# Product keys: one head's mask made on GpSimd from ScalarE's copy, four heads turned singly

## The chip, the cores and the metric

The kernel runs on one core of a Trainium2 chip. The metric is the device time of one execution in microseconds. A core has five engines with queues of their own: TensorE (PE; its weight loads are shown as PEld), VectorE (DVE), ScalarE (ACT), GpSimd (POOL) and SyncE (SP). They work in order, each on its own queue, and wait for each other by semaphores. Only TensorE writes the banks of PSUM here, GpSimd can't read them, and VectorE and ScalarE can.

## The reference

Twelve layers act one after the other on x, 2 x 1024 tokens of 128 numbers. The change touches the first and the third, which are the same layer, product keys:

```python
def _L0_ffn_ref(x, norm_w, wq, keys, expert_down, expert_up):   # HEADS 8, K 16, NUM_KEYS 32
    x_norm = x * rsqrt(mean(x * x) + EPS) * norm_w
    q = (x_norm @ wq).reshape(B, T, HEADS, 2, DIM_KEY)
    sim = einsum('bthpd,hkpd->pbthk', q, keys)
    s1, i1 = top_k(sim[0], K)
    s2, i2 = top_k(sim[1], K)
    all_scores = (s1[..., :, None] + s2[..., None, :]).reshape(B, T, HEADS, K * K)
    final_scores, pk = top_k(all_scores, K)
    final_idx = take_along_axis(all_idx, pk)
    hidden = gelu(einsum('btd,bthkd->bthk', x_norm, expert_down[final_idx]))
    hidden = hidden * relu(final_scores)
    return einsum('bthk,bthkd->btd', hidden, expert_up[final_idx])
```

The kernel gathers nothing. For each token and head it forms all 32 x 32 = 1024 sums of two similarities, finds the sixteenth best as a threshold, keeps the sums at or above it (a mask) and adds the eight heads' masked sums. The result, 1024 weights per token, multiplies the gelu of x times all of expert_down, and that goes through expert_up.

## The kernel before

The layer is `product_key_ffn`. It works on 16 tiles (`NT`) of 128 tokens, one after the other, and each engine has a `period(i, ...)` that lists its work for tile i in order, with the work for the tiles ahead and the tile behind in between. All order is written out by hand; loops (`Fori`) run over pairs of tiles, so that every second period of VectorE ends with a jump.

For one head h of tile i:

- TensorE, `sum_halves` (line 506): the 1024 sums, in the PSUM pair of banks h % 2. It waits until the mask of head h - 2 has read the pair.
- ScalarE, `read_sums` (620): copies the sums to `sums_sb`, buffer h % 2 (the trace's pk_sums).
- VectorE, `mask` (722): `chosen[h] = (sums in PSUM >= least2) * sums_sb`, one instruction.
- The heads are then added and turned on TensorE, `combine` (513): eight transposes per call accumulate in two banks. For heads 0 and 1, 2 and 3, 4 and 5, GpSimd adds two heads first, `pair` (425), and the sum is turned once; heads 6 and 7 are turned singly. That makes five calls per tile. ScalarE reads the result out, `read_added` (627), and GpSimd multiplies it by the gelus, `weight` (433).

For the threshold of tile i + 1, during tile i: VectorE finds the best keys of each head (`find_best`, 684, after masks 0 and 1), GpSimd forms the candidates (`add_candidates`, 406 to 419), VectorE finds the top eight (`find_top`, 700, after masks 3 and 4), takes them out (`leave_top_out`, 705, after masks 5 and 6), and after mask 7 `find_rest` finds the next eight (710) and writes the threshold:

```python
nc.vector.tensor_scalar(least2[:, odd, :], top[:, :, PK_TOP - 1], 0.0, PK_UNDER, ALU.max, ALU.mult)   # line 712
nc.vector.drain()
```

GpSimd's order in a period is: candidates of i + 1 (waits for the best keys of all heads), pair 0, weight of i - 1, take of i + 2 (394), pair 1, pair 2, low split of i + 2 (`split_low`, 399, which waits for ScalarE's copy of the similarities and feeds the transposes `turn`, 480, early in the next period).

## Time and profile before

| | us |
|---|---|
| median of 3 runs | 2503.75 (2501.33 to 2503.94) |
| the profiled execution | 2503.85, its span 2502.1 |
| first product-key stage | 48 to 355 |
| second product-key stage | 596 to 907 |
| busy in the whole span: PE, DVE, ACT, POOL | 2042.6, 1768.6, 1272.0, 1177.2 |
| mean granted TensorE clock | 0.912 |

The span is the time from the first to the last instruction. Busy times are of one execution. An instruction's start and duration are given in us from the start of the span; what stands in square brackets behind it is the idle time of the engine before it and what ended it. A granted clock of 1.00 is 2.4 GHz, one of 0.50 is 1.2 GHz.

### The profile page before, as it was taken

What the parts mean: (1) busy time and instruction counts of PE and PEld (TensorE: products, weight loads), DVE (VectorE), ACT (ScalarE), POOL (GpSimd) and SP (SyncE); (2) the same over time, 40 slices, a digit from 0 to 9 for tenths busy, and PEclk for the clock granted to TensorE, in tenths of its full rate; (3) what the DMA queues carried; (4) which work ended last, traced back from release to release, by engine and by line L of the source; (5) the groups of instructions that cost most, each with busy time, mean ns of one, the idle gap of its engine ahead of it and who ended that gap; (6) DMA issues with size and microseconds to landing.
All of it is one profiled execution on the core that took longest, in us unless ns stands there. A gap on an engine that the chain in (4) does not pass through costs nothing. (4 is left out here: it accounts for less than half of the span.)

```text
span 2502.1 us, 39069 instructions
## 1 busy us (share of the span) xinstructions
PE 2042.6 (82%) x11750; PEld 1625.5 (65%) x11775; DVE 1768.6 (71%) x4657; ACT 1272.0 (51%) x2389; POOL 1177.2 (47%) x1051
## 2 busy tenths in 40 slices
PE   4888859994888869976997998988983579999745
PEld 3666656663666658854886885667872468888634
DVE  4999953447999967657766765667667668787575
ACT  3666646653666645543555553335542257776321
POOL 3777751002776746531554653003541388887013
PEclk9999989996999979987997998998996789999978
DMA  3000000000000000001000000000000000000000
GB/s 110 1 0 0 0 15 1 0 0 0 1 0 0 0 1 1 1 5 54 1 1 1 1 1 27 1 6 4 1 1 0 1 10 4 5 6 0 19 0 17
DMA packets 16203, 18.64 MB, mean 7 GB/s; under 512 B 2208, under 2 KB 14048, under 8 KB 16096
## 3 DMA queue, kind: packets, MB, share of 16 engines
q1 hardware_dynamic: 16096, 17.35, 2.3%
q8 instruction: 50, 0.82, 0.1%
q14 instruction: 57, 0.47, 0.1%
HBM read 16.30 MB, written 1.05 MB: 7 GB/s over the span
## 5 line engine op out<-in xcount | busy, mean ns | idle before, releaser
L925 POOL TENSOR_TENSOR unit_hid_low<-unit_hid,unit_hid_high 128x512 fp32r<-128x512 f32 x272 | 351.6, 1293 | 329.9 <-ACT unit_hid_high L1103 329.3
L722 DVE SCALAR_TENSOR_TENSOR pk_chosen<-bank,pk_least,pk_sums 128x1024 f32<-128x1024 f32 x256 | 325.3, 1277 | 43.1 <-ACT pk_sums L620 26.0
L620 ACT COPY pk_sums<-bank 128x1024 f32<-128x1024 f32 x256 | 258.6, 1016 | 179.9 <-PE bank L506 174.8
L506 PE MATMUL bank<-pk_pick,pk_sim_both 128*128 128x512 f32 x512 | 197.3, 469 | 103.7 <-DVE pk_chosen L722 103.0
L425 POOL TENSOR_TENSOR pk_chosen<-pk_chosen 128x1024 f32<-128x1024 f32 x96 | 226.7, 2377 | 7.6 <-DVE pk_chosen L722 7.6
L978 PE MATMUL bank<-unit_x_high,units_high 128*128 128x512 f32 x544 | 219.2, 403 | 0.0
L979 PE MATMUL bank<-unit_x_low,units_high 128*128 128x512 f32 x544 | 218.5, 402 | 0.0
L980 PE MATMUL bank<-unit_x_high,units_low 128*128 128x512 f32 x544 | 217.8, 400 | 0.0
L1103 ACT CAST unit_hid_high<-unit_hid 128x512 fp32r<-128x512 f32 x272 | 167.2, 615 | 43.9 <-DVE unit_hid L1230 24.3
L506 PEld LDWEIGHTS bank<-pk_pick,pk_sim_both 128*128 128x128 f32 x512 | 82.5, 201 | 157.4 <-DVE pk_chosen L722 147.4
L513 PE MATMUL bank<-ident,pk_chosen 128*128 128x128 f32 x1280 | 175.0, 283 | 1.3 <-DVE pk_chosen L722 1.3
L513 PEld LDWEIGHTS bank<-ident,pk_chosen 128*128 128x128 f32 x1280 | 157.9, 146 | 23.9 <-issue 2.2
L1096 ACT ACTIVATE unit_gact<-bank,units_small 128x512 f32<-128x512 f32 x136 | 93.5, 689 | 124.3 <-PE bank L980 123.3
L1096 ACT ACTIVATE unit_gact<-bank 128x512 f32<-128x512 f32 x136 | 81.2, 599 | 128.4 <-PE bank L980 128.3
L1217 DVE SCALAR_TENSOR_TENSOR unit_prod<-bank,units_small,unit_gact 128x512 f32<-128x512 f32 x136 | 102.0, 750 | 62.4 <-ACT unit_gact L1096 60.2
L1220 DVE TENSOR_TENSOR unit_prod<-bank,unit_gact 128x512 f32<-128x512 f32 x136 | 93.9, 690 | 65.0 <-PE bank L980 62.1
L2670 POOL TENSOR_TENSOR dh_la<-dh_la_tok,causal 128x1024 fp32r<-128x1024 f32 x64 | 120.1, 1897 | 4.6
L1230 DVE SCALAR_TENSOR_TENSOR unit_hid<-unit_prod,units_small,bank 128x512 f32<-128x512 f32 x136 | 101.8, 748 | 29.0 <-PE bank L1013 24.3
L980 PEld LDWEIGHTS bank<-unit_x_high,units_low 128*128 128x128 f32 x544 | 105.3, 194 | 24.2
L979 PEld LDWEIGHTS bank<-unit_x_low,units_high 128*128 128x128 f32 x544 | 105.3, 194 | 24.0
L978 PEld LDWEIGHTS bank<-unit_x_high,units_high 128*128 128x128 f32 x544 | 105.6, 194 | 23.5
L1013 PE MATMUL bank<-unit_comb,units_pick 128*128 128x512 f32 x272 | 109.5, 405 | 7.1 <-DVE unit_comb L1203 7.1
(387 smaller groups left out, 5158.9 us busy)
## 6 DMA issues: line engine op xcount, KB each, us to landing
raw<-in_geglu_units SPq DMA_DIRECT2D x3, 774.0 KB, 7.5
raw<-in_swiglu_units SPq DMA_DIRECT2D x3, 768.0 KB, 7.6
dh_w_next<-in_de_w SPq DMA_DIRECT2D x8, 192.0 KB, 2.3
out_x<-x_res SPq DMA_DIRECT2D x1, 1024.0 KB, 5.1
raw<-in_geglu_units SPq DMA_DIRECT2D x1, 967.5 KB, 11.1
raw<-in_swiglu_units SPq DMA_DIRECT2D x1, 960.0 KB, 11.2
pk_down<-in_pk_downT SPq DMA_DIRECT2D x1, 512.0 KB, 5.2
pk_up<-in_pk_up SPq DMA_DIRECT2D x1, 512.0 KB, 6.5
```

The source lines that it names most:

```text
L425: nc.gpsimd.tensor_tensor(chosen[:, 2 * c, :], chosen[:, 2 * c, :], chosen[:, 2 * c + 1, :], ALU.add).then_inc(paired.sem, 1)
L506: ins = nc.tensor.matmul(sums_ps[:, 2 * b + e, :], both[:, odd, h, :], pk.pick[:, e * PK_K // 2:(e + 1) * PK_K // 2, :].rearrange("p i j - ...
L513: ins = nc.tensor.matmul(comb_ps[j // 4][:, (j % 4) * P:(j % 4 + 1) * P], chosen[:, h, j * P:(j + 1) * P], k.ident[:], start=(first and j ...
L620: nc.scalar.copy(sums_sb[:, b, :].rearrange("p (e n) -> p e n", e=2), sums_ps[:, 2 * b:2 * b + 2, :]).then_inc(sums_out.sem, 1)
L722: nc.vector.scalar_tensor_tensor(chosen[:, h, :].rearrange("p (e n) -> p e n", e=2), sums_ps[:, 2 * b:2 * b + 2, :], least2[:, odd, h:h + ...
L925: nc.gpsimd.tensor_tensor(hid_low[:, i % HB, :], hid[:, i % HB, :], hid_high[:, i % HB, :].bitcast(FP32), ALU.subtract).then_inc(hidden.se ...
L978: nc.tensor.matmul(to, w_hi, x_high[:, tokens], start=True, stop=False)
L979: nc.tensor.matmul(to, w_hi, x_low[:, tokens], start=False, stop=False)
L980: return nc.tensor.matmul(to, w_lo, x_high[:, tokens], start=False, stop=True)
L1096: nc.scalar.activation(gact[:, i % 2, :], gate_ps[i % 2], m.func, bias=b).then_inc(gated.sem, 1)
L1103: nc.scalar.copy(hid_high[:, i % HB, :], hid[:, i % HB, :]).then_inc(rounded.sem, 1)
L2670: ins = nc.gpsimd.tensor_tensor(la[:, q % 2, i, :, :, :].rearrange("p t h n -> p (t h) n"), la_tok[:, i, :, :].rearrange("p t h -> p (t h) ...
```

## The change

Head 4's mask leaves VectorE. ScalarE copies head 4's sums to a third buffer of `sums_sb`, and GpSimd makes the mask from that copy alone, in two instructions with a drain between (`mask_head`), behind a dummy addition of two elements and in the place of pair 2. Heads 4 and 5, which were added and turned once, are turned singly, which makes six `combine` calls per tile: heads 6 and 4 of the tile behind at head 0, head 7 at head 1, pair 0 at head 4, head 5 at head 6, pair 1 at head 7. The sums of head 6 now wait for ScalarE's copy of head 4 in place of a mask. The clearing of `least2` becomes a clearing of eight numbers of `top`. The waits count accordingly.

```diff
-PK_PAIRS = PK_H // 2
+PK_PAIRS = 2
+PK_POOL_HEAD = 4
+PK_MASKED = PK_H - 1
+PK_COMBINED = PK_H - PK_PAIRS
...
-        sums_sb = k.scratch(ctx, "pk_sums", [P, 2, PK_E])
+        sums_sb, unused = k.scratch(ctx, "pk_sums", [P, 3, PK_E]), k.scratch(ctx, "pk_unused", [P, 2])
...
+        buffer_of = lambda h: 2 if h == PK_POOL_HEAD else h % 2
+        masked_to = lambda i, h: PK_MASKED * i + (h + 1 if h < PK_POOL_HEAD else h)
...
+            def mask_head(i, odd):
+
+                if since(i, 1):
+                    pool.wait_ge(combined.sem, combined.at(PK_COMBINED * (i - 1) + 5))
+                pool.wait_ge(least_ready.sem, least_ready.at(i + 1))
+                pool.wait_ge(sums_out.sem, sums_out.at(PK_H * i + PK_POOL_HEAD + 1))
+                nc.gpsimd.tensor_tensor(unused[:], k.ones[:, 0:2], k.ones[:, 0:2], ALU.add)
+                nc.gpsimd.tensor_scalar(chosen[:, PK_POOL_HEAD, :], sums_sb[:, 2, :],
+                                        least2[:, odd, PK_POOL_HEAD:PK_POOL_HEAD + 1], None, ALU.is_ge)
+                nc.gpsimd.drain()
+                nc.gpsimd.tensor_tensor(chosen[:, PK_POOL_HEAD, :], chosen[:, PK_POOL_HEAD, :], sums_sb[:, 2, :],
+                                        ALU.mult).then_inc(masked_pool.sem, 1)
...
                 pair(i, 1)
-                pair(i, 2)
+                mask_head(i, odd)
...
-                if since(i, 1) or h >= 2:
-                    pe.wait_ge(masked.sem, masked.at(n - 1))
+                if h == PK_POOL_HEAD + 2:
+                    pe.wait_ge(sums_out.sem, sums_out.at(n - 1))
+                elif h >= 2:
+                    pe.wait_ge(masked.sem, masked.at(masked_to(i, h - 2)))
+                elif since(i, 1):
+                    pe.wait_ge(masked.sem, masked.at(masked_to(i - 1, PK_H + h - 2)))
...
                         if not first:
-                            combine_pair(i - 1, 2)
+                            combine_head(i - 1, PK_H - 2)
+                            combine_head(i - 1, PK_POOL_HEAD)
...
                     if h == 6:
-                        combine_head(i, PK_H - 2)
+                        combine_head(i, PK_POOL_HEAD + 1)
...
                 act.wait_ge(sums.sem, sums.at(PK_H * i + h + 1))
+                if h == PK_POOL_HEAD and since(i, 1):
+                    act.wait_ge(masked_pool.sem, masked_pool.at(i))
-                nc.scalar.copy(sums_sb[:, b, :].rearrange("p (e n) -> p e n", e=2),
+                nc.scalar.copy(sums_sb[:, buffer_of(h), :].rearrange("p (e n) -> p e n", e=2),
...
-                    nc.vector.memset(least2[:, odd, :], 0.0)
+                    nc.vector.memset(top[:, 0, 0:8], 0.0)
...
-                nc.vector.tensor_scalar(least2[:, odd, :], top[:, :, PK_TOP - 1], 0.0, PK_UNDER, ALU.max, ALU.mult)
+                nc.vector.tensor_scalar(least2[:, odd, :], top[:, :, PK_TOP - 1], 0.0, PK_UNDER, ALU.max,
+                                        ALU.mult).then_inc(least_ready.sem, 1)
...
                 for h in range(PK_H):
-                    mask(i, odd, h)
+                    if h != PK_POOL_HEAD:
+                        mask(i, odd, h)
```

## Rows read from the trace of the kernel before

**Rows 1.** Busy time by stage: window, length, each engine's busy us (instructions), clock, DMA

```profile
48.00:355.00 307.00, 249.26 (x1552) 205.24 (x1552) 270.10 (x909) 192.32 (x249) 213.18 (x182) 0.94 0.00 0
596.00:907.00 311.00, 249.97 (x1558) 204.76 (x1556) 274.94 (x943) 195.37 (x253) 214.49 (x184) 0.94 0.00 0
```

**Rows 2.** The page's costliest groups: count, busy us, mean ns, idle before

```profile
L722 DVE SCALAR_TENSOR_TENSOR pk_chosen<-bank,pk_least,pk_sums 128x1024 f32<-128x1024 f32 x256 | 325.3, 1277 | 43.1 <-ACT pk_sums L620 26.0
...
L425 POOL TENSOR_TENSOR pk_chosen<-pk_chosen 128x1024 f32<-128x1024 f32 x96 | 226.7, 2377 | 7.6 <-DVE pk_chosen L722 7.6
```

**Rows 3.** The timeline of VectorE, one period: start us, us, instruction, idle before

```profile
199.19 1.28 DVE L722 SCALAR_TENSOR_TENSOR pk_chosen<-bank,pk_least,pk_sums 128x1024 f32<-128x1024 f32 x1 [0.27 <-issue]
...
204.09 2.46 DVE L722 SCALAR_TENSOR_TENSOR pk_chosen<-bank,pk_least,pk_sums 128x1024 f32<-128x1024 f32 x2
...
209.45 1.28 DVE L722 SCALAR_TENSOR_TENSOR pk_chosen<-bank,pk_least,pk_sums 128x1024 f32<-128x1024 f32 x1
...
214.95 1.30 DVE L710 MAX8 pk_top<-pk_cand_rest 128x8 f32<-128x87 f32 x8
216.33 0.74 DVE L712 TENSOR_SCALAR pk_least<-pk_top 128x8 f32<-128x8 f32 x1
217.77 1.28 DVE L722 SCALAR_TENSOR_TENSOR pk_chosen<-bank,pk_least,pk_sums 128x1024 f32<-128x1024 f32 x1 [0.69 <-issue]
```

**Rows 4.** The timeline of GpSimd in the same period

```profile
203.25 0.63 POOL L406 TENSOR_TENSOR pk_cand<-pk_sims,pk_best 128x256 f32<-128x256 f32 x1 [4.36 <-DVE pk_best L684]
...
206.21 2.37 POOL L425 TENSOR_TENSOR pk_chosen<-pk_chosen 128x1024 f32<-128x1024 f32 x1
...
211.12 4.70 POOL L425 TENSOR_TENSOR pk_chosen<-pk_chosen 128x1024 f32<-128x1024 f32 x2
215.78 1.27 POOL L399 TENSOR_TENSOR pk_sim_parts<-pk_sims,pk_sim_parts 128x512 fp32r<-128x512 f32 x1
```

**Rows 5.** VectorE's groups up to 906 us, line 712

```profile
L712 DVE TENSOR_SCALAR pk_least<-pk_top 128x8 f32<-128x8 f32 x32 | 20.6, 643 | 2.5
```

**Rows 6.** The timeline at the end of the following period, all engines

```profile
235.32 1.28 POOL L399 TENSOR_TENSOR pk_sim_parts<-pk_sims,pk_sim_parts 128x512 fp32r<-128x512 f32 x1 [0.92 <-ACT pk_sim_parts L603]
...
235.97 0.66 DVE L712 TENSOR_SCALAR pk_least<-pk_top 128x8 f32<-128x8 f32 x1
...
236.90 1.28 DVE L722 SCALAR_TENSOR_TENSOR pk_chosen<-bank,pk_least,pk_sums 128x1024 f32<-128x1024 f32 x1 [0.27 <-issue]
```

**Rows 7.** The timelines of GpSimd and VectorE at the last threshold

```profile
324.10 4.72 POOL L425 TENSOR_TENSOR pk_chosen<-pk_chosen 128x1024 f32<-128x1024 f32 x2
...
329.57 0.17 DVE L712 TENSOR_SCALAR pk_least<-pk_top 128x8 f32<-128x8 f32 x1
330.05 1.28 DVE L722 SCALAR_TENSOR_TENSOR pk_chosen<-bank,pk_least,pk_sums 128x1024 f32<-128x1024 f32 x1 [0.30 <-ACT pk_sums L620]
```

**Rows 8.** The timeline of all engines, TensorE's and ScalarE's instructions

```profile
201.10 1.04 PE L513 MATMUL bank<-ident,pk_chosen 128*128 128x128 f32 x8
...
207.53 1.01 ACT L620 COPY pk_sums<-bank 128x1024 f32<-128x1024 f32 x1 [0.34 <-PE bank L506]
...
219.10 0.87 PE L506 MATMUL bank<-pk_pick,pk_sim_both 128*128 128x512 f32 x2 [1.92 <-DVE pk_chosen L722]
...
219.78 1.91 PE L513 MATMUL bank<-ident,pk_chosen 128*128 128x128 f32 x8
```

**Rows 9.** TensorE's granted clock by windows of 19 us (the second view: PE alone)

```profile
198.00:217.00 19.00, 15.88 (x109) 13.10 (x106) 18.01 (x63) 12.99 (x17) 14.49 (x13) 1.00 0.00 0
217.00:236.00 19.00, 15.78 (x95) 12.90 (x94) 16.70 (x61) 11.83 (x16) 13.15 (x13) 0.91 0.00 0
...
690.00:709.00 19.00, 15.77 (x97) 0.91 0.00 0
```

**Rows 10.** GpSimd's groups by shape: nearest prices

```profile
L412 POOL TENSOR_TENSOR pk_cand<-pk_best 128x64 f32<-128x64 f32 x64 | 18.0, 299 | 0.0
...
L1950 POOL COPY ro_xb<-x_norm_t 128x1024 f32 x2 | 2.1, 1038 | 13.7 <-PE bank L1974 13.7
...
L2542 POOL TENSOR_SCALAR_AFFINE_SELECT de_mask<-dg_zeros 128x512 bf16<-128x512 f32 x1 | 0.6, 634 | 0.2 <-issue 0.2
```

More of the change, by code:

```diff
@@ L39 @@
     pk_sums pk_sums_out pk_masked pk_paired pk_combined pk_added_out pk_hidden pk_gelu pk_weighted
-    pk_product pk_product_out pk_folded pk_scaled
+    pk_product pk_product_out pk_folded pk_scaled pk_masked_pool pk_least
 """, """
@@ L359, in product_key_ffn @@
              "pk_second", "pk_cand", "pk_sums", "pk_sums_out", "pk_masked", "pk_paired", "pk_combined", "pk_added_out",
-             "pk_hidden", "pk_gelu", "pk_weighted", "pk_product", "pk_product_out")
+             "pk_hidden", "pk_gelu", "pk_weighted", "pk_product", "pk_product_out", "pk_masked_pool", "pk_least")
     (tile_in, sim, sim_out, sim_high, sim_low, sim_t, sim_t_out, best_ready, second, cand_ready, sums, sums_out, masked,
-     paired, combined, added_out, hidden, gelu, weighted, product, product_out) = [k.counter(n) for n in names]
+     paired, combined, added_out, hidden, gelu, weighted, product, product_out, masked_pool, least_ready) = [k.counter(n) for n in names]
     NCH = PK_E // P
@@ L422, in pair @@
             def pair(i, c):
-                pool.wait_ge(masked.sem, masked.at(PK_H * i + 2 * c + 2))
+                pool.wait_ge(masked.sem, masked.at(masked_to(i, 2 * c + 1)))
                 nc.gpsimd.tensor_tensor(chosen[:, 2 * c, :], chosen[:, 2 * c, :], chosen[:, 2 * c + 1, :],
                                         ALU.add).then_inc(paired.sem, 1)
+            def mask_head(i, odd):
[9 more added lines that the diff above has]
+                                        ALU.mult).then_inc(masked_pool.sem, 1)
             def weight(i, odd):
@@ L519, in combine_pair @@
             def combine_pair(i, c):
-                pe.wait_ge(paired.sem, paired.at((PK_PAIRS - 1) * i + c + 1))
+                pe.wait_ge(paired.sem, paired.at(PK_PAIRS * i + c + 1))
                 if c == 0:
@@ L526, in combine_head @@
             def combine_head(i, h):
-                pe.wait_ge(masked.sem, masked.at(PK_H * i + h + 1))
+                if h == PK_POOL_HEAD:
+                    pe.wait_ge(masked_pool.sem, masked_pool.at(i + 1))
+                else:
+                    pe.wait_ge(masked.sem, masked.at(masked_to(i, h)))
                 combine(h, last=(h == PK_H - 1))
@@ L592, in _ @@
             period(NT - 1, 1, last=True, ahead=False)
-            combine_pair(NT - 1, 2)
+            combine_head(NT - 1, PK_H - 2)
+            combine_head(NT - 1, PK_POOL_HEAD)
             combine_head(NT - 1, PK_H - 1)
@@ L717, in mask @@
                 b = h % 2
-                if since(i, 1) and h in (0, 2, 4, 7):
-                    dve.wait_ge(combined.sem, combined.at((PK_PAIRS + 1) * (i - 1) + {0: 1, 2: 3, 4: 4, 7: 5}[h]))
+                if since(i, 1) and h in (0, 2, 6, 7):
+                    dve.wait_ge(combined.sem, combined.at(PK_COMBINED * (i - 1) + {0: 1, 2: 3, 6: 4, 7: 6}[h]))
                 dve.wait_ge(sums_out.sem, sums_out.at(n + 1))
@@ L765, in product_key_ffn @@
         s.passed(NT)
-    for s in (sums, sums_out, masked):
+    for s in (sums, sums_out):
         s.passed(NT * PK_H)
-    paired.passed(NT * (PK_PAIRS - 1))
-    combined.passed(NT * (PK_PAIRS + 1))
+    masked.passed(NT * PK_MASKED)
+    for s in (masked_pool, least_ready):
+        s.passed(NT)
+    paired.passed(NT * PK_PAIRS)
+    combined.passed(NT * PK_COMBINED)
     for s in (sim_t, sim_t_out, hidden, gelu):
```

2 lines of the change are left out of this document (1 added, 1 removed).

## The prediction

> **What bounds the kernel now.** I read the stages first. The change touches only the two product-key stages, and together they take 618 of the 2502 us of span [rows 1]. In both VectorE is the busiest engine (270 of 307 us, 275 of 311 us), so the page invites the sentence "VectorE sets the pace". The groups of the page give the prices: one head mask on VectorE 1277 ns, one pair sum on GpSimd 2377 ns [rows 2]. A tile has eight masks and three pair sums.
>
> Next the timeline of one tile in the steady part, engine by engine. I count from the start of the tile's mask 0, at 199.19; all times written +x are us after it. The next tile's mask 0 starts at 217.77, so this period is 18.58 us [rows 3]. VectorE has little idle time in it; 0.69 us of it lie before the next mask 0. GpSimd starts the candidates at +4.06, as soon as the eighth head's best keys are there, then runs without a pause through pair 0, weight, take, pair 1, pair 2 and the low split, which it starts at +16.59 and ends at 217.05, +17.86 [rows 4].
>
> The reader is to look at what stands at that time on VectorE: the small operation on line 712, the threshold of the next tile, starts at 216.33 and ends at 217.07, with the end of GpSimd's split. It handles 128x8 elements. Of its 32 instances the mean is 643 ns [rows 5]. In the following period it ends at 236.63 and the split ends at 236.60 [rows 6]. Near the end of the stage there is no split, GpSimd has been idle since 328.82, and line 712 takes 0.17 us [rows 7]. So it holds off until GpSimd's running instruction is over, and this costs some 0.57 us here, beyond its own work. The masks (one input in PSUM) last 1.27 to 1.28 us beside a busy or an idle GpSimd [rows 2 to 4]: they don't wait in this way. The Trainium skill, "SBUF — State Buffer", section "Who interferes with whom", has this as an exclusive lock of a shared port pair, taken for a whole instruction by a VectorE tensor_scalar in a two-port mode or by a GpSimd instruction, whichever was first; the 0.17 against 0.74 us agree.
>
> The period is thus closed by a loop over two engines: mask 0, best keys, GpSimd's whole queue, line 712, mask 0. VectorE without that hold would be done with line 712 at +17.31 (starts at +17.14, lasts 0.17), GpSimd lets it go at +17.88.
>
> A third thing is TensorE's clock. It idles 1.92 us before the first sums of the next tile at 219.10, so since 217.18, and then runs at its low level (1.2 GHz): eight turns take 1.91 us, 1.04 at the high one (2.4 GHz) [rows 8]. A stretch of this kind shows as 0.91 in a window of 19 us, and one without it as 1.00; six tiles of the first stage have one and five of the second [rows 9]. A period with such a stretch is 19.13 us (217.77 to 236.90): line 712 starts at +18.20 in it instead of +17.14 [rows 6].
>
> **VectorE's part of the change.** Mask 4 goes: -1.28 us per tile, 32 tiles, 41 us, were VectorE alone the bound. It isn't all to be had even there. Mask 5 needs ScalarE's copy of head 5, which ran at 207.53 to 208.54 [rows 8], and in front of that copy the work of the extra turn (below) moves ScalarE's queue some 0.3 us later. So mask 5 can start at about +9.65 in place of +10.26 [rows 3], the rest follows at its old spacing, and line 712 is ready to start at about +16.55 (+17.14 less 0.6). The fill of the top tile's first eight numbers in place of the threshold's is the same small memset: nothing.
>
> **GpSimd's part.** One pair sum goes (2.38 us). In come a dummy addition of 2 elements, the compare, a drain and a multiplication. The multiplication has the pair sum's shape and inputs: 2.37. The dummy: 64 elements take 0.30 us [rows 10], back to back less; 0.2. The drain: 0.15, my estimate from steps between GpSimd's small instructions; both may be off by 0.1 together. The compare has one tensor input, and no row shows a tensor_scalar on GpSimd. Lower bound: the copy of 128x1024, 1.04 us; upper: the two-input rate, 2.38 [rows 2, 10]. The one other compare, the affine select of 128x512, takes 0.63 us, about 1.1 for twice the elements, so I take 1.05 for start to start. New is then 3.77 for 2.38, the queue grows by 1.4 us per tile. GpSimd is idle for 4.36 us before the candidates [rows 4], so by load alone this is free.
>
> By place it isn't. Pair 1 ends, and the dummy starts, at +14.28 (211.12 + 2.35). Dummy to +14.48, compare to +15.53, drain to +15.68, multiplication to +18.05. Line 712 becomes ready at +16.55, in the middle of the multiplication, and must stand until +18.05. Before, it was let go at +17.88. The mask taken off VectorE gives nothing: its 0.6 us turn into more waiting on the same loop, and the loop is 0.17 us longer. In sentences of their own: the same page's rule, that the second to come waits for the whole instruction, and the skill's warning in "Perfetto Trace Analysis", section "Optimizing Scalar/DVE Operations", that moving work between these two engines might not help because they share a port, both speak against this change. By load without the rule the stages would lose some 1.2 us per period.
>
> **TensorE's part.** Six groups of eight turns per tile for five: +0.87 us of issue. The two turned singly at head 0 come before the turns of the similarities and before the sums of head 3, so these are 0.87 us later. At the high clock this is covered: the sums of head 3 end at about +4.9, ScalarE's copy about +6.0, and mask 3 starts at +6.1 anyway, back to back behind mask 2 at 204.09, +4.90 [rows 3]. At the low clock it isn't. The chain from the first sums to the sums of head 4 is 0.87 us longer and its 0.1 us of slack is left in place of 1; the 1.7 us that a low stretch costs TensorE come through whole, where before 1.06 did (18.20 less 17.14): mask 5 is as late as before, and line 712 gets ready at about +18.17, no earlier than today's +18.20. By then the multiplication is over (+18.05) and the low split has begun: it holds line 712 until about +19.3. Before: +18.86. So a period with a low stretch is 0.4 us longer. The gap in which TensorE idles grows too (last multiplications over at +17.4, next sums at +19.7 to +20.1: 2.3 to 2.7 us for about 1.4, without a low stretch after it, and 1.9, with one), which speaks for at least as many low stretches. The head 6 sums wait for ScalarE's copy and not for a mask: earlier, covered. ScalarE's copy of head 4 waits for the last tile's multiplication, done by +0.1 of its period: nothing. No DMA is moved.
>
> **The sum.** Between line 712's end and mask 0 lie 0.69 us at a loop's end, else 0.27 [rows 3, 6]. Thirteen periods per stage are in the steady part, six with the loop's end. Before, in the first stage: 7 x 18.17 (17.88 + 0.02 + 0.27) + 6 x 18.58 + 6 x 0.96 for low stretches (19.13 less 18.17) = 244.4; in the second, with five, 243.5. After: 7 x 18.34 + 6 x 18.76 = 240.9, and low stretches that come out at 19.55 or 19.97, +1.21 each; I take five to six of them, +6.5: 247.4, so +3.0 and +3.9 us. The next to last tile has no split, and line 712 lasted 0.17 us there [rows 7]; now it waits for the multiplication to +18.05: +0.7 each. The last tile: its final turns wait for GpSimd's last product, about where the last pair sum ended: 0 to 0.3. Sum: 3.0 + 3.9 + 1.4 + 0.3, about +8.6 us. Against the profiled execution: span 2502.1, time 2503.85 (1.75 around it), the median 2503.75. Forecast 2512.
>
> **The rivals.**
> *The compare is slow enough to let line 712 through (faster).* If it takes 1.95 us or more, the multiplication hasn't begun when line 712 is ready; line 712 goes between them, at about +16.87 with a compare of 2.37, and mask 0 follows at +17.14 or +17.56. TensorE's gap falls to 1.1 to 1.5 us, so no low stretches. 7 x 17.14 + 6 x 17.56 = 225.3, 19 us less per stage: 2465. It decides at +16.55. For: the two-input rate of all the neighbours. Against: copy and select at about 1 ns per element.
> *The product doesn't hold line 712 (faster).* The same gain, about 2464. Against it: in 28 of the 32 instances line 712 ended with GpSimd's instruction, and in the other four GpSimd was idle [rows 3 to 7].
> *A compare of 1.3 to 1.9 us (slower).* Every 0.1 us moves the multiplication's end, and the loop, by 0.1 us. At 1.85 the loop is at +18.85, 0.95 us over before, and low stretches hide in it: 13 x 19.3 = 251, +7 per stage, +1.6 each for the next to last tile: 2521. The Trainium skill, "GPSIMD Engine Reference", section "Performance pitfalls for Q7 kernels", has compare bodies at 2.03 cycles per element unless unrolled, 1.03 if so; by its figures an estimate of the compare would be 1.8 or 0.95 us.
> *Nothing to be measured.* Line 712 in low stretches gets ready by +18.0 instead of +18.17 and slips in ahead of the split. Then these cost nothing, 2 x (241 + 0.7) against 488: about 2500 to 2505.
>
> **How the numbers follow.** The forecast's case 0.36, the slower compare 0.17, nothing to be measured 0.22, the two faster ones 0.25 (0.20 and 0.05). About 0.2% (5 us) is what a measurement of this kernel tells from no change. The likeliest case has 2505 to 2518 as its range. Both signs hold much of the chance, so the range goes from the fast compare to the slow one: 2463 to 2526. Slower 0.53, same 0.22, faster 0.25.
>
> **What the profile will show.** Right: line 712 ends with the end of GpSimd's multiplication, with a mean duration near 1.5 us and not 0.64; mask 5 starts about 0.6 us earlier in the tile, mask 0 no earlier; VectorE's busy time apart from line 712 falls by 41 us and the span does not. The compare is between 1.0 and 1.15 us. Low stretches at half of the tiles or more, with line 712 ending with the low split. Wrong: if line 712 ends ahead of the multiplication, I have mis-sized the compare or VectorE's chain; if it ends inside it, the hold is not what I take it for; if TensorE idles at the turn of head 4 at the tile's start, waiting for GpSimd's product, the wait is on another engine than I say.

## The result and the profile after

The changed kernel takes 2527.53 us (median of 5 runs, 2517.78 to 2531.99), the one before 2502.9 (5 runs, 2495.05 to 2503.94): ratio 1.0103, 95% interval 1.0075 to 1.0131. It is slower by 1.0%, 24.6 us by these medians, where 2512 was forecast, and just above the range forecast (2463 to 2526). The profiled execution has a span of 2525.8 us.

The page's costliest groups and its total of busy time (engine, busy us, share, instructions):

```profile
PE 2072.3 (82%) x12006; PEld 1663.4 (66%) x12031; DVE 1757.3 (70%) x4625; ACT 1263.8 (50%) x2389; POOL 1275.7 (51%) x1115
...
L752 DVE SCALAR_TENSOR_TENSOR pk_chosen<-bank,pk_least,pk_sums 128x1024 f32<-128x1024 f32 x224 | 285.0, 1276 | 78.7 <-ACT pk_sums L649 64.5
```

GpSimd's groups up to 935 us, by shape:

```profile
L440 POOL TENSOR_SCALAR pk_chosen<-pk_sums,pk_least 128x1024 f32<-128x1024 f32 x32 | 91.2, 2851 | 0.0
...
L443 POOL TENSOR_TENSOR pk_chosen<-pk_chosen,pk_sums 128x1024 f32<-128x1024 f32 x32 | 75.3, 2354 | 4.7
```

VectorE's groups up to 935 us, the threshold (line 712 before, 741 now):

```profile
L741 DVE TENSOR_SCALAR pk_least<-pk_top 128x8 f32<-128x8 f32 x32 | 47.6, 1486 | 2.5
```

Against [rows 2, 5]: 32 masks are gone from VectorE, 325.3 to 285.0 us, as the change says, and the idle time ahead of the masks rose from 43.1 to 78.7. The threshold rose from 643 to 1486 ns, 27 us in all, for 128x8 elements each time. And the compare, line 440, takes 2851 ns, not the 1.05 us that I took, and longer than either of my bounds. The product (2354 ns) is as forecast.

The timeline of the changed kernel, one period of the first stage from mask 0 at 209.72 to mask 0 at 230.33, 20.61 us, for [rows 3, 4, 8] (start us, us, instruction, idle before it):

```profile
209.72 1.28 DVE L752 SCALAR_TENSOR_TENSOR pk_chosen<-bank,pk_least,pk_sums 128x1024 f32<-128x1024 f32 x1 [0.29 <-issue]
...
211.05 0.73 PE L528 MATMUL bank<-pk_pick,pk_sim_both 128*128 128x512 f32 x2 [2.69 <-DVE pk_chosen L752]
...
211.62 3.45 PE L535 MATMUL bank<-ident,pk_chosen 128*128 128x128 f32 x16
...
220.81 1.28 DVE L752 SCALAR_TENSOR_TENSOR pk_chosen<-bank,pk_least,pk_sums 128x1024 f32<-128x1024 f32 x1 [0.92 <-ACT pk_sums L649]
...
224.08 0.20 POOL L439 TENSOR_TENSOR pk_unused<-ones 128x2 f32<-128x2 f32 x1
...
224.25 2.85 POOL L440 TENSOR_SCALAR pk_chosen<-pk_sums,pk_least 128x1024 f32<-128x1024 f32 x1
...
227.25 2.35 POOL L443 TENSOR_TENSOR pk_chosen<-pk_chosen,pk_sums 128x1024 f32<-128x1024 f32 x1
...
227.70 1.92 DVE L741 TENSOR_SCALAR pk_least<-pk_top 128x8 f32<-128x8 f32 x1
229.55 1.27 POOL L404 TENSOR_TENSOR pk_sim_parts<-pk_sims,pk_sim_parts 128x512 fp32r<-128x512 f32 x1
230.33 1.28 DVE L752 SCALAR_TENSOR_TENSOR pk_chosen<-bank,pk_least,pk_sums 128x1024 f32<-128x1024 f32 x1 [0.71 <-issue]
```

The product begins at 227.25, the threshold becomes ready at 227.70, 0.45 us too late, and ends with the product (229.60 and 229.62). Sixteen turns take 3.45 us, against 1.91 in the period below, so TensorE began this tile at its low level (1.2 GHz). I call that a low start; a high start is one at 2.4 GHz.

The same kernel in the second stage, from mask 5 to the end of one period, and the mask 0 that follows, with TensorE's rows behind it:

```profile
671.39 1.28 DVE L752 SCALAR_TENSOR_TENSOR pk_chosen<-bank,pk_least,pk_sums 128x1024 f32<-128x1024 f32 x1 [0.67 <-ACT pk_sums L649]
...
676.39 2.85 POOL L440 TENSOR_SCALAR pk_chosen<-pk_sums,pk_least 128x1024 f32<-128x1024 f32 x1
...
678.27 0.99 DVE L741 TENSOR_SCALAR pk_least<-pk_top 128x8 f32<-128x8 f32 x1
679.38 2.35 POOL L443 TENSOR_TENSOR pk_chosen<-pk_chosen,pk_sums 128x1024 f32<-128x1024 f32 x1
679.98 1.28 DVE L752 SCALAR_TENSOR_TENSOR pk_chosen<-bank,pk_least,pk_sums 128x1024 f32<-128x1024 f32 x1 [0.72 <-issue]
...
681.32 0.73 PE L528 MATMUL bank<-pk_pick,pk_sim_both 128*128 128x512 f32 x2 [1.90 <-DVE pk_chosen L752]
681.88 1.91 PE L535 MATMUL bank<-ident,pk_chosen 128*128 128x128 f32 x16
```

Mask 0 before that is at 661.95, so the period is 18.03 us. The threshold is ready 16.32 us into it, while the compare still runs. It is held for 0.99 us, but it gets in at the compare's end (679.24), ahead of the product. Mask 5 starts 9.44 us into this period (10.26 before) and 11.09 into the one above. The kernel thus has two modes, and TensorE's granted clock tells them apart. In the first mode every tile has a low start and the product holds the threshold, in the second every tile has a high start and only the compare does. The first two windows below lie in the first mode (0.91), the last two in the second (1.00); columns are length, TensorE's busy us with instructions, clock, DMA:

```profile
120.00:140.00 20.00, 16.86 (x107) 0.91 0.00 0
200.00:220.00 20.00, 16.85 (x107) 0.91 0.00 0
...
660.00:680.00 20.00, 17.22 (x122) 1.00 0.00 1
700.00:720.00 20.00, 17.40 (x125) 1.00 0.00 0
```

| | before | after, second mode | after, first mode |
|---|---|---|---|
| period, us (alternating) | 18.17 / 18.58; 19.13 with a low start | 17.61 / 18.02 | 20.2 / 20.6 |
| threshold ready, us into it | 17.15; 18.21 low | 16.32 | 17.98 |
| threshold done | 17.89; 18.87 low | 17.32 | 19.90 |

All of the first stage's steady part is in the first mode: thirteen periods, from mask 0 at 67.16 to mask 0 at 332.05, in 264.9 us, where the kernel before took 244.6. The second stage has eight periods in the second mode (644.34 to 786.86, 17.8 on average) and then changes over for good: its thirteen take 244.3 us, before 243.4. The threshold of the next to last tile, which before lasted 0.17 us [rows 7], is held for 1.57 by the product in both stages, and that period is 2.3 us longer. The last tile is 1.1 us longer in the first stage and 1.9 in the second: its final turns wait 1.56 and 1.57 us for GpSimd's product of head 4 (until 368.50 and 925.08). The stages, from the first mask 0 to the addition behind the last tile, are 329.3 and 308.9 us long where they were 305.5 and 303.9: +23.8 and +5.0. The rest of the kernel is 5 us shorter in this execution, which makes the +23.7 of the spans. That the same kernel ran between 2517.8 and 2532.0 us fits a changeover that comes earlier or later from run to run; only one of those runs has a profile, so this is argued and not shown.

### The profile page after: what moved, and what is told of

Its sections match the earlier page's. It is cut to its first block and busy times, and to the rows that moved or that the text cites. A ratio compares the mean times of both kernels' runs of the same rounds, so it can differ in the third digit from the quotient of the medians.

```text
span 2525.8 us, 39661 instructions
## 1 busy us (share of the span) xinstructions
PE 2072.3 (82%) x12006; PEld 1663.4 (66%) x12031; DVE 1757.3 (70%) x4625; ACT 1263.8 (50%) x2389; POOL 1275.7 (51%) x1115
## 3 DMA queue, kind: packets, MB, share of 16 engines
HBM read 16.30 MB, written 1.05 MB: 7 GB/s over the span
## 5 line engine op out<-in xcount | busy, mean ns | idle before, releaser
L752 DVE SCALAR_TENSOR_TENSOR pk_chosen<-bank,pk_least,pk_sums 128x1024 f32<-128x1024 f32 x224 | 285.0, 1276 | 78.7 <-ACT pk_sums L649 64.5
L535 PE MATMUL bank<-ident,pk_chosen 128*128 128x128 f32 x1536 | 222.8, 299 | 3.1 <-POOL pk_chosen L443 3.1
L535 PEld LDWEIGHTS bank<-ident,pk_chosen 128*128 128x128 f32 x1536 | 203.2, 156 | 26.5 <-issue 3.7
L430 POOL TENSOR_TENSOR pk_chosen<-pk_chosen 128x1024 f32<-128x1024 f32 x64 | 152.1, 2376 | 5.8 <-DVE pk_chosen L752 5.8
L1013 PEld LDWEIGHTS bank<-unit_x_low,units_high 128*128 128x128 f32 x544 | 105.2, 193 | 23.8
```

The costliest lines, as they stand in the source:

```text
L430: nc.gpsimd.tensor_tensor(chosen[:, 2 * c, :], chosen[:, 2 * c, :], chosen[:, 2 * c + 1, :], ALU.add).then_inc(paired.sem, 1)
L535: ins = nc.tensor.matmul(comb_ps[j // 4][:, (j % 4) * P:(j % 4 + 1) * P], chosen[:, h, j * P:(j + 1) * P], k.ident[:], start=(first and j ...
L752: nc.vector.scalar_tensor_tensor(chosen[:, h, :].rearrange("p (e n) -> p e n", e=2), sums_ps[:, 2 * b:2 * b + 2, :], least2[:, odd, h:h + ...
L1013: nc.tensor.matmul(to, w_hi, x_low[:, tokens], start=False, stop=False)
```

## The experiments

Each edit is against the changed kernel unless it says that it is against the one before. Ratios, with 95% intervals, are to the kernel before as it was timed anew beside each group of runs. It took 2500.45 us beside the threshold on ScalarE, the product in four pieces, the twelve multiplications and the turns alone; 2504.29 beside the same threshold in the kernel before, the prices, the compare left out and the eight multiplications; and 2500.29 beside the rest.

### Is it the hold? The threshold on ScalarE

```diff
-                nc.vector.tensor_scalar(least2[:, odd, :], top[:, :, PK_TOP - 1], 0.0, PK_UNDER, ALU.max,
-                                        ALU.mult).then_inc(least_ready.sem, 1)
...
+            def threshold(i, odd):
+
+                act.wait_ge(rest_ready.sem, rest_ready.at(i + 1))
+                nc.scalar.activation(least2[:, odd, :], top[:, :, PK_TOP - 1], ACT.Relu,
+                                     scale=PK_UNDER).then_inc(least_ready.sem, 1)
...
+                    if h == 7 and not last:
+                        threshold(i + 1, 1 - odd)
...
+                if h == 0:
+                    dve.wait_ge(least_ready.sem, least_ready.at(i + 1))
```

The threshold becomes the last instruction of a tile on ScalarE's queue, behind the copy of head 7, and VectorE's mask 0 waits for it.

> The changed kernel, with the threshold (max with 0, times a constant) computed by ScalarE from VectorE's top sixteen, so that no VectorE instruction at this place can be held by GpSimd; compare and product stay as long as they are. Theory A (the hold is what turns GpSimd's queue into time): in low stretches mask 0 follows at about +18.6 or +19.0 in place of +20.2 or +20.6, at the high clock at about +17.0 or +17.4; time 2480 to 2500. Rival B (it is the length of GpSimd's queue, through TensorE waiting for head 4's product or the low split): at least 2515, with TensorE idle in front of head 4's turns.

Measured: 2459.98 us, ratio 0.9840 (0.9820 to 0.9860), better than expected. The timeline of this kernel at the end of a period and the start of the next:

```profile
218.20 2.87 POOL L440 TENSOR_SCALAR pk_chosen<-pk_sums,pk_least 128x1024 f32<-128x1024 f32 x1
...
220.64 0.22 ACT L655 ACTIVATE pk_least<-pk_top 128x8 f32<-128x8 f32 x1
221.07 1.29 DVE L760 SCALAR_TENSOR_TENSOR pk_chosen<-bank,pk_least,pk_sums 128x1024 f32<-128x1024 f32 x1 [0.78 <-ACT pk_least L655]
221.22 2.37 POOL L443 TENSOR_TENSOR pk_chosen<-pk_chosen,pk_sums 128x1024 f32<-128x1024 f32 x1
```

The threshold takes 0.22 us in the middle of GpSimd's compare, and mask 0 starts while GpSimd still has the product to do. Every period of the steady parts is 17.2 to 17.3 us, and no low start is left in them. TensorE never waits for head 4's product there; it does so for 1.55 us in the last tile of each stage. The same edit on the kernel before:

> The kernel before with the one edit of act_after: the threshold is computed by ScalarE. Theory A (GpSimd's low split holds line 712 in the kernel before too, and the changed kernel only lengthens that hold): mask 0 comes at about +17.6 in place of +18.17 and +18.58, TensorE's gap is down to about 1.0 us, so no low stretches; time 2470 to 2480. With it, the worth of the changed kernel's edit free of the hold can be read: act_after's periods were 17.24 us. Rival B (the hold is a cost of the changed kernel alone): 2495 to 2502.

Measured: 2474.32 us, ratio 0.9878 (0.9850 to 0.9905); periods 17.77 and 17.83. So the kernel before, too, had some 30 us to gain. They aren't all the hold. The steady parts of the two stages are 25.4 us shorter (231.5 and 231.1 for 244.6 and 243.4). Eleven low starts that are gone make 10.5 of it; some 5 are the jump at the end of VectorE's loop, which made every second period 0.41 us longer and doesn't show now that mask 0 waits for ScalarE; some 10, about 0.4 us a period, are the hold, net of ScalarE's 0.26 us until it starts the threshold. The edit also takes two drains off VectorE, which no run tests by themselves.

With the threshold on ScalarE in both, the change is to the good, by some 10 us. The medians differ by 14 us (2474 and 2460) but were timed beside different runs of the kernel before; the ratios (0.9878 and 0.9840) give 9.5 us, and their intervals just overlap. In the profiles the steady parts are 14.0 us shorter together, and the last tiles 3.2 longer.

### What holds it? The product in four pieces, and the threshold in eight

```diff
-                nc.gpsimd.tensor_tensor(chosen[:, PK_POOL_HEAD, :], chosen[:, PK_POOL_HEAD, :], sums_sb[:, 2, :],
-                                        ALU.mult).then_inc(masked_pool.sem, 1)
+                for part in range(4):
+                    at = slice(part * PK_E // 4, (part + 1) * PK_E // 4)
+                    ins = nc.gpsimd.tensor_tensor(chosen[:, PK_POOL_HEAD, at], chosen[:, PK_POOL_HEAD, at],
+                                                  sums_sb[:, 2, at], ALU.mult)
+                ins.then_inc(masked_pool.sem, 1)
```

> The changed kernel, with the product on GpSimd in four pieces of 256 columns (about 0.65 us each, 0.2 to 0.3 us more in sum). Theory A (whole instructions hold, VectorE comes in at the end of one): the threshold ends with the piece in which it became ready, at most 0.7 us after +17.98, so low periods of about 18.9 and 19.3, time about 2500 or less. Rival B (GpSimd's queue has to end before the threshold gets in): as the changed kernel or 0.3 us per period over it, 2527 to 2535.

Measured: 2492.29 us, ratio 0.9967 (0.9952 to 0.9982). The timeline where the threshold is late:

```profile
225.92 2.78 POOL L445 TENSOR_TENSOR pk_chosen<-pk_chosen,pk_sums 128x256 f32<-128x256 f32 x4
226.38 0.30 DVE L744 TENSOR_SCALAR pk_least<-pk_top 128x8 f32<-128x8 f32 x1
226.97 1.28 DVE L755 SCALAR_TENSOR_TENSOR pk_chosen<-bank,pk_least,pk_sums 128x1024 f32<-128x1024 f32 x1 [0.29 <-ACT pk_sums L652]
```

The four products together take longer (2.78 for 2.35 us), yet the threshold, 0.46 us behind their start as before, lasts 0.30 us for 1.92: it waits for one piece and not for the product. A period with a low start is 18.56 us in place of 20.2. TensorE's gap behind such a period is only about 1.07 us, and the next tile starts high: seven of the 26 steady periods have a low start, and never two in a row. So with the hold cut short the first mode doesn't lock. One steady period (18.94 us, behind one of 16.79) has TensorE waiting 0.86 us for head 4's product at the tile's start, the wait that the prediction named as its third sign of being wrong; it is the only one in the steady parts of these runs. The other side of the same question: eight thresholds of one column each.

```diff
-                nc.vector.tensor_scalar(least2[:, odd, :], top[:, :, PK_TOP - 1], 0.0, PK_UNDER, ALU.max,
-                                        ALU.mult).then_inc(least_ready.sem, 1)
+                for h in range(PK_H):
+                    ins = nc.vector.tensor_scalar(least2[:, odd, h:h + 1], top[:, h, PK_TOP - 1:PK_TOP], 0.0, PK_UNDER,
+                                                  ALU.max, ALU.mult)
+                ins.then_inc(least_ready.sem, 1)
```

> The changed kernel with the threshold computed on VectorE as before, but in eight instructions of one column each in place of one of eight columns. Theory A (the hold comes with the form that streams one operand through both of VectorE's ports, and one element has no second half): none of the eight is held, each takes 0.07 us or so, the threshold is done by +16.9 at the high clock, periods 17.2 to 17.7, time 2462 to 2480. Rival B (any tensor_scalar from SBUF to SBUF is held, or each of the eight anew between GpSimd's instructions): durations of over 1 us among them, time as the changed kernel or more, 2515 or over.

Measured: 2480.22 us, ratio 0.9912 (0.9886 to 0.9937), at the upper edge of what I expected of theory A (2462 to 2480). The timeline, first a tile with a low start, where the product runs from 85.56 to 87.91, then one with the compare running from 224.67 to 227.52:

```profile
85.56 2.35 POOL L443 TENSOR_TENSOR pk_chosen<-pk_chosen,pk_sums 128x1024 f32<-128x1024 f32 x1
...
86.03 0.58 DVE L742 TENSOR_SCALAR pk_least<-pk_top 128x1 f32<-128x1 f32 x8
...
224.67 2.85 POOL L440 TENSOR_SCALAR pk_chosen<-pk_sums,pk_least 128x1024 f32<-128x1024 f32 x1
...
226.56 0.58 DVE L742 TENSOR_SCALAR pk_least<-pk_top 128x1 f32<-128x1 f32 x8
227.52 1.28 DVE L754 SCALAR_TENSOR_TENSOR pk_chosen<-bank,pk_least,pk_sums 128x1024 f32<-128x1024 f32 x1 [0.38 <-ACT pk_sums L649]
```

Eight instructions on the same engine do the same work in 0.58 us, 0.47 us behind the product's start, where one instruction, 0.45 us behind it, takes 1.92 in the changed kernel. Two low starts are left, in the first steady tile of each stage, and they don't lock. The threshold on VectorE is not held as such: it is this instruction of eight columns that is. The Trainium skill, "SBUF — State Buffer", section "Who interferes with whom", has a VectorE tensor_scalar contend for the port pair shared with GpSimd when it runs in a two-port mode. That a one-column instruction stays out of that mode would fit the page, but no row shows the mode.

### The price of the compare

The kernel before with seven GpSimd instructions added at its end, each three times, in sequence and with no other engine at work:

> The kernel before with a stage added at its end, in which GpSimd alone runs seven operations three times each, on 128x1024 but for one: a copy, is_ge with a constant, is_ge with a per-token threshold, the same on 128x512, a multiplication by a per-token number, is_ge and mult with constants in one instruction, and a subtraction of two tensors. Theory A (the price is that of the compare): the two is_ge forms about 2.85 us, the multiplication about 1.04 us like the copy. Rival B (the price is that of reading the scalar from memory): is_ge with a constant about 1.04, the multiplication about 2.85. Rival C (the price is that of tensor_scalar on GpSimd): all four near 2.85. 512 columns: 1.4 us if it goes by columns.

The timeline of GpSimd in that part:

```profile
2493.86 1.04 POOL L3174 COPY pr_copy<-pr_src 128x1024 f32<-128x1024 f32 x1
2494.87 2.78 POOL L3175 TENSOR_SCALAR pr_imm<-pr_src 128x1024 f32<-128x1024 f32 x1
2497.64 2.84 POOL L3176 TENSOR_SCALAR pr_ptr<-pr_src,pr_lim 128x1024 f32<-128x1024 f32 x1
2500.46 1.56 POOL L3177 TENSOR_SCALAR pr_half<-pr_src,pr_lim 128x512 f32<-128x512 f32 x1
2502.00 2.85 POOL L3178 TENSOR_SCALAR pr_mul<-pr_src,pr_lim 128x1024 f32<-128x1024 f32 x1
2504.82 3.64 POOL L3179 TENSOR_SCALAR pr_two<-pr_src 128x1024 f32<-128x1024 f32 x1
2508.43 1.89 POOL L3180 TENSOR_TENSOR pr_sub<-pr_src 128x1024 f32<-128x1024 f32 x1
```

A compare costs what a multiplication with a per-token value costs (2.84, 2.85), and a constant in place of the value saves 0.06. So neither the compare nor the read of the threshold is what makes it dear, and the other engines don't either: on GpSimd, this tensor_scalar costs 2.7 times the copy, and 1.2 times a product of two tensors. Half the columns take 1.56 us and not 1.42, so by these two rows about 0.3 us of it doesn't go by columns (my estimate). Then the compare left out, with head 4's product kept (this kernel leaves the mask of head 4 out, so it is for timing alone):

```diff
-                nc.gpsimd.tensor_scalar(chosen[:, PK_POOL_HEAD, :], sums_sb[:, 2, :],
-                                        least2[:, odd, PK_POOL_HEAD:PK_POOL_HEAD + 1], None, ALU.is_ge)
-                nc.gpsimd.drain()
-                nc.gpsimd.tensor_tensor(chosen[:, PK_POOL_HEAD, :], chosen[:, PK_POOL_HEAD, :], sums_sb[:, 2, :],
+                nc.gpsimd.tensor_tensor(chosen[:, PK_POOL_HEAD, :], sums_sb[:, 2, :], sums_sb[:, 2, :],
```

> The changed kernel without the compare and its drain: GpSimd multiplies head 4's sums with themselves, so head 4's mask is left out. The hold, the extra turn and the third buffer stay. Theory A (it is the size of the compare, 2.85 us, that puts the product where it holds a late threshold): the product runs from about +14.5 to +16.85, periods about 17.1 and 17.6 us at the high clock, low ones at most 19.1; time 2460 to 2480. Rival B (the extra turn and the low clock make the loss): 2510 or more.

Measured: 2490.6 us, ratio 0.9945 (0.9932 to 0.9959), less gain than expected. The timeline shows why:

```profile
138.35 1.90 POOL L440 TENSOR_TENSOR pk_chosen<-pk_sums 128x1024 f32<-128x1024 f32 x1
...
140.21 1.28 POOL L404 TENSOR_TENSOR pk_sim_parts<-pk_sims,pk_sim_parts 128x512 fp32r<-128x512 f32 x1
140.25 1.27 DVE L738 TENSOR_SCALAR pk_least<-pk_top 128x8 f32<-128x8 f32 x1
```

The queue is shorter by more than the compare, since the product with both inputs the same takes 1.90 us and not 2.35. The product is over at +16.32, just as the threshold gets ready, and the next instruction, the low split, starts 0.04 us ahead of the threshold and holds it for 1.27 in the product's place. In the nine steady periods with a low start (18.9 us) the split holds it too, 0.66 us. Taking work off GpSimd does not remove the hold: what counts is which instruction happens to start just ahead of the threshold.

### TensorE's clock

Zero multiplications into a PSUM bank whose values they don't alter, in TensorE's gap ahead of the next tile's first sums: twelve and then five of them in the changed kernel, eight in the one before. In a trace each shows as two passes.

```diff
+            def fill():
+                for _ in range(12):
+                    nc.tensor.matmul(low_ps[:, 0:P], nothing[:], k.ident[:], start=False, stop=False)
...
-                            multiply(i - 1, (5, 6, 7))
+                            multiply(i - 1, (5, 6))
+                            fill()
+                            multiply(i - 1, (7,))
```

> The changed kernel, with twelve multiplications of a zero tile added on TensorE in the stretch in which it waits for the next tile's threshold (they add zero to a sum that is open anyway). Theory A (the threshold on VectorE is held by GpSimd's product only because the low TensorE clock has made it late: ready at +17.98, the product begins at +17.53; without the low clock it is ready at +16.32 and passes at the compare's end, +17.32): no low stretches in the steady part, every period 17.6 or 18.0 us as in the first eight periods of the second stage, steady part of the first stage from 265 to about 231 us, of the second from 244 to 231; time about 2480, some 1% under the kernel before. Rival B (GpSimd's queue, longer by 3 us, sets the period whatever the clock): periods stay at 20.2 and 20.6, time 2520 to 2530.

Measured: 2503.0 us, ratio 1.0011 (1.0001 to 1.0022). The clock is 1.00 throughout the steady part, and the locked 20.2 us periods are gone, but not the 2480 that I expected. The timeline:

```profile
212.05 2.35 POOL L444 TENSOR_TENSOR pk_chosen<-pk_chosen,pk_sums 128x1024 f32<-128x1024 f32 x1
...
212.39 2.04 DVE L750 TENSOR_SCALAR pk_least<-pk_top 128x8 f32<-128x8 f32 x1
...
212.86 2.84 PE L572 MATMUL bank<-ident,pk_nothing 128*128 128x128 f32 x24
```

The fill lasts 2.8 us, longer than the gap, so that the sums come later with each period: the threshold is ready at 16.32, 17.25, 17.36, 17.80 us in turn. The fourth one falls behind the product's start at the high clock and is held 2.04 us; near the end of the first stage one starts 0.02 us behind the product and takes 2.37, the longest in these runs. It isn't the clock that holds, but lateness; the low clock is one way to be late. With five:

> As awake_after with five multiplications of the zero tile in place of twelve, because each of them takes two passes and twelve took 2.8 us, longer than TensorE's gap at the high clock (1.5 us) and so late themselves; five take about 1.2 us. Theory A (a threshold that is ready before the compare is over passes; the low clock is what makes it late in the changed kernel): no low stretches but perhaps in the first tile, the threshold ready at +16.3, every period 17.6 or 18.0, time 2475 to 2485. Rival B (GpSimd's backlog, 1.2 us over per fast period, comes back by way of the low split and makes a threshold late every few tiles, as in awake_after, without any low clock): some periods of 20.5 remain, time 2495 to 2505.

Measured: 2481.75 us, ratio 0.9919 (0.9897 to 0.9942), as expected. All steady periods of both stages are 17.6 or 18.0 us; the timeline has the threshold end with the compare each time:

```profile
223.09 2.86 POOL L441 TENSOR_SCALAR pk_chosen<-pk_sums,pk_least 128x1024 f32<-128x1024 f32 x1
...
224.99 0.98 DVE L750 TENSOR_SCALAR pk_least<-pk_top 128x8 f32<-128x8 f32 x1
...
225.74 1.28 PE L572 MATMUL bank<-ident,pk_nothing 128*128 128x128 f32 x10
226.09 2.37 POOL L444 TENSOR_TENSOR pk_chosen<-pk_chosen,pk_sums 128x1024 f32<-128x1024 f32 x1
```

So 1.3 us of work without use turns the change from 1.0% slower to 0.8% faster. On the kernel before:

> The kernel before with eight multiplications of a zero tile (about 1.0 us) in TensorE's gap. Theory A (its low stretches cost 0.96 us each, eleven in the two stages): every period 18.17 or 18.58, time 2490. Rival B (the added work delays TensorE's next sums as in awake_after, where the threshold was ready at +17.25 in place of +16.32): 2500 or more, with the threshold ready later than +17.15.

Measured: 2502.78 us, ratio 0.9999 (0.9984 to 1.0014). The low starts are gone there too, and the steady parts of the two stages are shorter by 10 us together (238.8 and 238.7 for 244.6 and 243.4), but the median doesn't follow. In the profiled execution the part of the kernel behind the second stage is 5.5 us longer (1602.6 for 1597.1). That part is the same code in all of these kernels but the one with the prices, and its length goes from 1592.4 us (the changed kernel) to that 1602.6, with 1601.9 in a run without any added multiplication (the turns alone), so the 5.5 us need not come of the added work. Why the medians of ten and seventeen runs lie 1.5 us apart and not 10, these runs don't settle.

### The turns alone, and GpSimd's queue

Against the kernel before, pair 2 goes and heads 4 and 5 are turned singly, with all eight masks on VectorE:

```diff
-                pair(i, 2)
...
-                            combine_pair(i - 1, 2)
+                            combine_head(i - 1, 6)
+                            combine_head(i - 1, 4)
...
-                        combine_head(i, PK_H - 2)
+                        combine_head(i, 5)
```

> One part of the change alone, on the kernel before: heads 4 and 5 are turned singly and pair 2 is gone, but all eight masks stay on VectorE. Theory A (the extra turn in front of the similarities' turns costs time only in low stretches): at the high clock the period is 18.0 or 18.4 us (the low split now ends at about +17.75), with a low stretch 19.7 to 20.2 where it was 19.13, because the threshold gets ready some 0.8 us later and the split has moved with ScalarE's copy; time 2497 to 2512. Rival B (the extra turn is covered everywhere): 19.13 stays 19.13 or less, time 2495 to 2502. Rival C (the extra turn makes the changed kernel's loss by itself): about 2525.

Measured: 2503.72 us, ratio 1.0014 (1.0000 to 1.0028), no change to speak of, and within theory A's range. The threshold is ready at +17.45 where it was at +17.15, and the split starts later too; periods are 18.37 and 18.79 (+0.2), against which only one low start is left in each stage's steady part (20.04 us, 0.9 over the 19.13 of before: the extra turn whole). The timeline there:

```profile
233.43 1.28 POOL L400 TENSOR_TENSOR pk_sim_parts<-pk_sims,pk_sim_parts 128x512 fp32r<-128x512 f32 x1 [4.07 <-ACT pk_sim_parts L605]
234.09 0.66 DVE L714 TENSOR_SCALAR pk_least<-pk_top 128x8 f32<-128x8 f32 x1
```

GpSimd had 4.07 us to spare and still held the threshold. Last, the version with the threshold on ScalarE and the copy of the tile (0.3 us) moved from GpSimd to ScalarE as well:

```diff
-                if ahead:
-                    take(i + 2, odd)
...
+                        if ahead:
+                            nc.scalar.copy(xt[:, odd, :], k.xnT[:, bass.ts(i + 2, P)]).then_inc(tile_in.sem, 1)
```

> act_after with one more edit: the copy of the next tile's tokens (0.29 us, 0.25 start to start) goes from GpSimd to ScalarE. Theory A (with the hold gone, GpSimd's queue of some 17.0 us is what sets act_after's 17.24 us): periods about 17.0 us, 7 us less in all, time about 2453. Rival B (VectorE's own chain or TensorE's sums set it): 17.24 stays, time 2460, or more by ScalarE's added 0.25 us in front of a sums copy.

Measured: 2464.21 us, ratio 0.9851 (0.9829 to 0.9873); not the 2453 of theory A. The periods stay at 17.2 to 17.3, but for one low start at the beginning (18.67), though the compare now ends at +17.05 in place of +17.30. Once the threshold is not held, GpSimd's queue doesn't set the period. This version and the one without the copy moved are the fastest, 1.5 and 1.6% under the kernel before, and their intervals overlap. Against the changed kernel the 2459.98 us are 2.7% less (from 2527.53, timed at another time).

## Why the prediction was wrong, step by step

**The steps that failed** are two, and the loss needs both. The first is the compare's price: "The compare has one tensor input [...] Lower bound: the copy of 128x1024, 1.04 us; upper: the two-input rate, 2.38". It measured 2.85 us, and 2.78 to 2.85 with no other engine at work. I took two rows of other operations for bounds, and they weren't bounds: the operation with one tensor input costs more than the one with two. Had I left the upper end open, I should have asked what 3 us would do. In a sentence by itself: the estimate of 0.95 or 1.8 us from the figures of the Trainium skill, "GPSIMD Engine Reference", section "Performance pitfalls for Q7 kernels" (its 1.03 or 2.03 cycles per element at that page's clock of 1.2 GHz come to 0.88 or 1.73), is as far off, and the measurement decides.

The price alone doesn't give the loss. With 2.85 us in my own sum the threshold passes at the compare's end, +17.33, and thirteen periods of 17.60 and 18.02 without low starts make 231.3 us a stage, about 2479 in all, faster than before; the run with five zero multiplications, which is just that case, took 2481.75. The second step that failed is what the rival of the slow compare goes on with: "TensorE's gap falls to 1.1 to 1.5 us, so no low stretches". The gap was 1.48 and 1.90 us in turn in the second mode, and one of 1.89 was followed by a low start. For a compare as long as this I priced neither that gap nor a hold by the product behind a low start.

**What the price did.** The product started at +17.5 and not at +15.68. I had worked out that a compare of 1.95 us or more lets the threshold through, and put that on the faster side, 2465. At the high clock this is what happened: ready at +16.32 (I had +16.55), done at the compare's end, +17.32, periods of 17.61 and 18.02. In a low period the threshold is ready at +17.98 (I had +18.17), 0.45 us behind the product's start, and is held to +19.90. A period is 20.2 or 20.6, where I had 19.55 or 19.97 for a hold by the split.

**The number of low starts.** I took five to six in thirteen periods. It was thirteen in the first stage and five in the second, and the first mode keeps itself going: the hold makes mask 0 late, TensorE idles 2.69 and then 3.12 us ahead of the sums (1.92 before, [rows 8]), starts low, so the next threshold is late and is held again. The run with the product in four pieces bears this out: held for one piece, a low period is never followed by another. I had 247.4 us for the steady part of either stage; it was 264.9 in the first, and 244.3 in the second, where eight short periods pay for five long ones. For the next to last tile I had +0.7 and it was +2.3, for the last 0 to 0.3 and it was 1.1 and 1.9. What I named as speaking "for at least as many low stretches" was the gap of 2.3 to 2.7 us; what it would do to the next tile I didn't price.

**Right.** That the threshold is held for the length of GpSimd's running instruction and sets the period: with it on ScalarE, both kernels gain, and with the product in pieces or the threshold in eight, the changed one does. That VectorE's 41 us aren't to be had: its masks fell by 40.3 us while the threshold rose by 27 and the idle time ahead of the masks by 35.6. That the 0.87 us of turns come through whole after a low start: ready is 1.66 us later there (17.98 less 16.32), where before it was 1.06, and I had 1.7. The small costs (0.20 us for the dummy instruction, some 0.15 for the drain, 2.35 for the product). The turns are not quite covered at the high clock, as the run with them alone shows: +0.3 us on the threshold, about what I had given to ScalarE's copy.

**Right by luck.** The side, slower: the case that I put there (a compare of 1.05 us, the product holding at every clock, +0.17 us a period) didn't occur, and the compare that did occur I had on the faster side. And the sign "a mean duration near 1.5 us" for the threshold: it was 1.49, but as a mixture of about 1.0 and 1.92, with none near 1.5 but the 1.57 of the next to last tiles. The sign of being wrong that came true is the first that I named, line 712 ending ahead of the multiplication, in the eight periods of the second mode.

**Of the rivals,** the slow compare that lets the threshold through came true in the second mode, and the first mode has the forecast's hold by the product, though only behind a low start, and for longer. The time is a mixture: in this execution 18 steady periods in the first mode and 8 in the second.

**Open.** What decides when the second mode changes over. The period from 768.84 to 786.86 looks like the seven before it, and TensorE's gap behind it, below, like the one at 681.32 (1.90 us, and sixteen turns in 1.91).

```profile
788.19 0.86 PE L528 MATMUL bank<-pk_pick,pk_sim_both 128*128 128x512 f32 x2 [1.89 <-DVE pk_chosen L752]
788.86 3.47 PE L535 MATMUL bank<-ident,pk_chosen 128*128 128x128 f32 x16
```

No run shows why one started low and the other didn't. The kernel before has the same: 1.98 us at 106.91 and a high start, 1.92 at 219.10 and a low one. In the profiles of this document but that of the prices, the first and last tile of each stage left out, the low starts stand behind gaps of 1.82 to 3.14 us, and the high ones behind gaps of up to 2.30.

## What to carry to other kernels

Before moving work between VectorE and GpSimd, look for a small VectorE instruction whose duration varies and whose end falls on the end of a GpSimd instruction; if it is on the loop that sets the period, give it to ScalarE or to a form that isn't held first, and only then count what the move saves. A price that no row shows has no upper bound from other operations: measure it alone, or carry the case above your bound through the loop. And when a wait makes TensorE's gap longer and a low start makes the wait, price the two as a loop that keeps itself going, and not the single stretch.

## What the runs showed of the hardware

GpSimd's tensor_scalar on 128x1024 float32 takes 2.8 us with one operation and 3.64 with two, against 1.04 for a copy, 1.89 for a difference of a tensor with itself and 2.35 for a product of two tensors. VectorE's threshold of 128x8 takes 0.17 us free and up to 2.37 held by a product of 2.35, and it gets in at the end of the running GpSimd instruction, between two of the four pieces too, which stand back to back; in eight pieces of one column it took 0.58 us beside a running compare and beside a running product. TensorE had gaps of 1.89 and 1.90 us ahead of two tiles alike in all else that I compared, and ran the sixteen turns behind them in 3.47 us after one and 1.91 after the other.
